# Another order of the steps in each round of the first stage, on four engines

## The reference

```
def bitlinear(x, w, g):
    xn = rmsnorm(x, g)
    xq = ste(xn, act_quant)        # per row: 127 / max|xn|, rounded to integers
    wq = ste(w, weight_quant)      # the weights become -1, 0 or 1, by one scale
    return jnp.einsum('bsd,od->bso', xq, wq)
y = bitlinear(layernorm(x), w_gate, g_gate)        # 512 -> 2 * 1408
gate, v = jnp.split(y, 2, axis=-1)
z = bitlinear(gate * sigmoid(gate) * v, w_down, g_down)      # 1408 -> 512
x = x + z
```

## Time and profile before

| | |
|---|---|
| median of 3 runs | 937.57 us (936.64 to 939.38) |
| profiled execution: span from the first to the last instruction | 967.5 us |
| busy PE, DVE, ACT, POOL over the span | 79%, 52%, 41%, 27% |
| mean granted clock of PE over the span | 0.912 |
| first stage, profiled | to 275.1 us (end of the last `h_lo`) |

### The profile page before, as it was taken

How to read it: one execution, slowest core, us unless ns; L and a number is a source line. 1 busy time by engine, 2 the same in 40 slices (tenths; PEclk the granted TensorE clock), 3 DMA queues, 4 the chain that set the end, 5 groups by cost and what they waited for, 6 DMA issues and landing times.

```text
span 967.5 us, 17562 instructions
## 1 busy us (share of the span) xinstructions
PE 760.4 (79%) x5001; PEld 452.5 (47%) x5017; DVE 504.4 (52%) x861; ACT 397.7 (41%) x567; POOL 263.6 (27%) x401
## 2 busy tenths in 40 slices
PE   0457777777429999749778998899999999999275
PEld 0234443444215555335445655566666666665133
DVE  6779888887714555446564567222222222222146
ACT  5866556656515555335343543122332223231010
POOL 1235665565321111032121000111111111104710
PEclk9979899888559999969898999899999999999679
DMA  9312222212544555267776542122222222226843
GB/s 353 112 34 77 61 70 87 87 66 87 158 159 135 180 179 179 95 209 238 230 215 216 201 148 78 56 88 87 76 77 86 87 78 77 84 77 224 248 138 138
DMA packets 51204, 127.57 MB, mean 132 GB/s; under 512 B 6496, under 2 KB 6496, under 8 KB 50528
## 3 DMA queue, kind: packets, MB, share of 16 engines
q1 hardware_dynamic: 42688, 99.33, 30.5%
q0 software_dynamic: 8480, 27.79, 9.9%
HBM read 87.78 MB, written 39.32 MB: 131 GB/s over the span
## 4 chain that ended last, share of the span: by engine, by line
PE 47%; DMA 10%; issue 4%; another core or an unknown queue 4%; DVE 4%; SPq 2%; ACT 1%; POOL 0%; DVEq 0%; POOLq 0%; ACTq 0%
PE banks L1338 41%; DMA x_d<-w_hi 5%; PE banks L1330 3%; PE banks L1428 2%; DMA x_d<-yrow 2%; DMA hC_d<-w_lo 1%; PE banks L1360 1%; DMA rows<-hC_d 1%; DVE w_hi L1246 0%; DMA rows<-hC_d,idx 0%; SPq L458 0%; SPq L441 0%; DVE w_lo L1102 0%; DMA rows<-hB_d,idx 0%
## 5 line engine op out<-in xcount | busy, mean ns | idle before, releaser
L1338 PE MATMUL banks<-w_hi,hT 128*128 (+1 forms) x1288 | 321.0, 326 | 4.4 <-issue 3.2
L1338 PE MATMUL banks<-w_lo,hT 128*128 (+1 forms) x644 | 209.8, 326 | 0.0
L1338 PEld LDWEIGHTS banks<-w_hi,hT 128*128 128x128 f16 x1288 | 128.0, 99 | 82.2 <-issue 10.6
L1338 PE MATMUL banks<-w_hi,cpT 128*128 (+1 forms) x426 | 142.9, 390 | 10.0 <-issue 8.6
L1299 PE MATMUL banks<-w_hi,w_lo 128*128 128x352 bf16 x384 | 89.3, 350 | 45.6 <-DVE w_hi L1015 34.3
L844 ACT ACTIVATE cs<-banks 128x352 f32<-128x352 f32 x71 | 32.9, 463 | 201.7 <-PE banks L1338 175.5
L1160 DVE TENSOR_TENSOR cs<-banks,cs 128x352 f32<-128x352 f32 x71 | 37.1, 523 | 140.9 <-ACT cs L844 135.0
L1164 DVE TENSOR_TENSOR cpT<-banks,cpT 128x384 f16<-128x384 f32 x71 | 39.5, 556 | 129.3 <-ACT cpT L849 112.6
L1338 PE MATMUL banks<-w_lo,cpT 128*128 (+1 forms) x213 | 83.1, 390 | 5.3 <-issue 5.3
L1330 PE MATMUL banks<-eyeH,rows 128*128 128x128 f16 x584 | 47.6, 225 | 48.2 <-DMA rows<-hC_d 19.6
L1338 PEld LDWEIGHTS banks<-w_lo,hT 128*128 128x128 f16 x644 | 63.9, 99 | 34.5 <-issue 0.8
(11 more groups left out here) (191 smaller groups left out, 1214.3 us busy)
## 6 DMA issues: line engine op xcount, KB each, us to landing
wstage<-in_wmoe SPq DMA_DIRECT2D x40, 544.0 KB
yC_d<-yrow SPq DMA_DIRECT2D x39, 256.0 KB, 2.0
w_hi<-x_d SPq DMA_DIRECT2D x20, 256.0 KB
yB_d<-yrow SPq DMA_DIRECT2D x19, 256.0 KB, 2.0
w_hi<-in_wgate SPq DMA_DIRECT2D x3, 1408.0 KB, 9.9
w_hi<-in_x SPq DMA_DIRECT2D x16, 256.0 KB, 2.8
w_lo<-in_x SPq DMA_DIRECT2D x16, 256.0 KB, 3.6
x_d<-w_lo SPq DMA_DIRECT2D x16, 256.0 KB, 2.9
```

The costliest lines, as they stand in the source:

```text
L1338: mm = pe.matmul(to, a(k, pa), w(k, pw), start=(begins and k == 0 and n == 0), stop=(ends and k == steps - 1 and n == 2))
```

## The change

Four lists are written in another order: those of POOL, ACT, DVE and PE for the first stage. SP's is as before. The steps, their tiles, their waits and their buffers are the same; the place of the second stage's weight chunks in the lists of ACT and DVE moves too.

```diff
@@ POOL
-            pipeline(pool, T, [(-2, small_x), (1, small_g), (3, small_b), (0, lambda s: gains(s, 0)),
-                               (0, lambda s: gains(s, 1)), (3, h_lo)])
+            pipeline(pool, T, [(-2, small_x), (3, small_b), (1, small_g), (0, lambda s: gains(s, 0)), (3, h_lo),
+                               (0, lambda s: gains(s, 1))])
@@ ACT
-            stages = [(0, lambda s: silu(s, 0)), (2, d_evac), (0, lambda s: silu(s, 1)), (1, square), (-1, dequant_x),
-                      (0, lambda s: silu(s, 2)), (-1, x_evac), (-2, x_round), (1, dequant_g),
-                      (0, lambda s: silu(s, 3)), (1, d_round), (3, h_hi)]
+            stages = [(0, lambda s: silu(s, 0)), (1, square), (0, lambda s: silu(s, 1)), (2, d_evac), (-1, dequant_x),
+                      (1, dequant_g), (1, d_round), (0, lambda s: silu(s, 2)), (-1, x_evac), (-2, x_round), (3, h_hi),
+                      (0, lambda s: silu(s, 3))]
-            pipeline(act, T, stages[:8] + [ctx_chunks(ctx_split)] + stages[8:], begin=CTX_FROM)
+            pipeline(act, T, stages[:10] + [ctx_chunks(ctx_split)] + stages[10:], begin=CTX_FROM)
@@ DVE
-            stages = [(3, residual1), (0, lambda s: swiglu(s, 0)), (1, g_absmax), (-3, x_spread),
-                      (0, lambda s: swiglu(s, 1)), (-1, x_int), (3, spread1), (-3, x_moments), (-2, x_reciprocal),
-                      (3, moments1), (-2, x_factor), (0, lambda s: swiglu(s, 2)), (1, g_reciprocal), (3, norm1),
-                      (1, g_factor), (-3, x_center), (0, lambda s: swiglu(s, 3)), (-3, x_absmax), (1, d_int)]
+            stages = [(3, residual1), (0, lambda s: swiglu(s, 0)), (3, spread1), (3, moments1), (1, g_absmax),
+                      (0, lambda s: swiglu(s, 1)), (-3, x_spread), (-3, x_moments), (1, g_reciprocal), (1, g_factor),
+                      (-2, x_reciprocal), (-2, x_factor), (-1, x_int), (3, norm1), (0, lambda s: swiglu(s, 2)), (1, d_int),
+                      (-3, x_center), (-3, x_absmax), (0, lambda s: swiglu(s, 3))]
@@ PE
             stages = [(0, lambda s: gate_up(s, 0)), (0, lambda s: gate_up(s, 1)), (2, d_turn),
-                      (0, lambda s: gate_up(s, 2)), (2, down), (-1, x_turn), (0, lambda s: gate_up(s, 3))]
+                      (0, lambda s: gate_up(s, 2)), (-1, x_turn), (2, down), (0, lambda s: gate_up(s, 3))]
```

## The result

The changed kernel takes **967.0 us** (median of 4 runs, 965.77 to 970.45) against 937.1 for the one before on the same chip (4 runs, 934.96 to 939.38): 1.0316 times as long, with a 95% interval of 1.0287 to 1.0346. The prediction was 961, within 934 to 975, with 0.72 for slower.

A forecast was written before the change was run, and what follows sets the result against it. The prediction took a cycle of waits to set the round, now through a late `x_int` and idle PE. Rounds and stage end gave -0.5 us, the clock +24: 937.6 + 23.5 = 961 us, range 934 to 975.

The forecast's parts named there:

- The walk of the cycle: First-stage round: `x_int`, held by `gains` 0, ends at 7.8 us, PE idles from 3.3; 13.15 us at full clock against 13.18.
- The clock: PE's clock falls after each round's 4.5 us idle piece, over `down` and `gate_up` 3: 2.0 us a round, +24 in all.
- A: Rival: DVE's relief sets the first-stage round at about 11.6 us, 915 us in all; chance 0.17, including a part of it.
- B: Rival: the walk holds but PE's clock does not fall, or falls only where it did before: 937 us; chance 0.12.
- C: Rival: `x_int` is not held, the round is 0.8 us shorter, the clock still falls: 951 us; chance 0.10.
- D: Rival: the whole PE chain runs at half clock, 6.7 us low each round: 974 us; chance 0.13 with what lies near.
- The sum: First-stage parts together -0.5 us without the clock, +24 for the clock: +23.5 us, later stages only moved.
- round 1: First stage's first round: `x_int` now waits for `small_g` and `gains` 0 too, while the clock is low: about +2.5 us.
- round 2: First stage's second round, without `small_b`: 12.2 us against 11.21, +1.0, plus half a clock loss for a shorter idle piece.
- rounds 3 to 12: First stage's middle rounds: 131.5 us at full clock against 131.33, +0.2 with the clock left out.
- rounds 13 to 15: First stage's last rounds, two without `small_x` or `x_int`: 37.1 us against 36.73, +0.4 without the clock.
- after the last `swiglu` 3: End of the first stage: its first piece falls from 15.4 us to about 10.8, -4.6; the 16.8 of loads stays.

The follow-up runs named there:

- e3: Changed kernel with 34 unused matmuls of 256 columns ahead of `x_turn`'s wait for `x_int`, from tile 2 on: 941.9 us, 1.005 times the kernel before.
- e1: Changed kernel with `x_int` moved behind `x_moments` on DVE, ahead of the wait for `small_g`: 926.3 us, 0.987 times the kernel before.
- e2: Changed kernel with `down` ahead of `x_turn` on PE, as in the kernel before: 922.8 us, 0.984 times the kernel before.
- e9: e7 with `swiglu` 3 right behind `swiglu` 2 on DVE, and ACT's `x_evac` and `h_hi` ahead of `silu` 2: 981.0 us, 1.012 times the kernel before.
- e7: Changed kernel with the edits of e1 and e2, and `norm1` ahead of the wait for `small_g`: 951.2 us, 0.982 times the kernel before.
- e4: Kernel before with `x_int` moved from behind `swiglu` 1 to behind `g_factor` on DVE: 982.6 us, 1.046 times the kernel before.
- e5: Kernel before with `x_turn` ahead of `down` on PE: 966.5 us, 0.997 times the kernel before.
- e11: Changed kernel timed again, unaltered, on the chip of e9: 998.6 us, 1.031 times the kernel before.

## Why the prediction was right

**The walk of the cycle** ended with `x_int` at 7.8 us after `swiglu` 3; the trace has 7.99. The hold was 0.29 beyond the `gains` (0.27 expected), `x_int` 1.20 (1 to 1.4), PE's idle piece 4.82 (4.5). The round at full clock was forecast as 13.15 and e3 measured 13.22. This was the step on which all else stood, and e1 and e2 show that it was the cause, since either way out of it removes the whole loss. The Trainium skill ("SBUF — State Buffer", section "Who interferes with whom") says that the later of the two instructions is blocked until the earlier one is through. The trace agrees for `x_int`, which started 0.76 us into the `gains` and ended 0.29 after it, while the `gains` kept its 1.67. It does not agree for `x_center` in e9: there the `gains` had started first and still took 2.05.

**The clock** was priced at 2.0 us a round; e3 gives 2.08. That this is so close is in part luck: 2.0 was a choice between 0 and 4, made for one kind of round, and there are two. The rounds take 14.7 to 14.8 and 15.9 in turn, some 1.6 and 2.7 over e3's, and 2.08 is the mean of the eight. `down` takes 3.50 us in the shorter, as in one of them (timeline of PE), and 4.47 in the longer, as above:

```profile
151.33 0.61 PE L1285 MATMUL banks<-w_lo 128*128 128x128 bf16 x4 [4.83 <-DVE w_lo L1007]
152.15 3.50 PE L1316 MATMUL banks<-w_lo 128*128 128x512 bf16 x10 [0.22 <-issue]
```

**The rivals.** A, that DVE's relief sets the round at 11.6, fell with the rounds of 15.3. With PE's wait out of the way (e2) the round is 11.83, near its number, but not shown to be so for its reason: e7 frees DVE of the last held `norm1`, DVE is busy 9.5 us a round there, and the round stays at 11.91. B fell with the clock at 0.83. C fell with `x_int` at 1.20. D's 974 would need rounds near 16.2; they are 15.3.

**The sum**, part by part, in us (before, after, difference, and what was forecast):

| part | before | after | difference | forecast |
|---|---|---|---|---|
| round 1 | | | +3.5 | +2.5 |
| round 2 | 11.21 | 14.93 | +3.7 | +2.0 |
| rounds 3 to 12 | 131.33 | 153.36 | +22.0 | +20.2 |
| rounds 13 to 15 | 36.73 | 42.68 | +5.95 | +3.4 |
| after the last `swiglu` 3 | 32.74 | 26.50 | -6.2 | -4.6 |
| first stage | | | +28.95 | +23.5 |

The measured time is 6 us above the forecast, 5.5 of them in this table: four parts were put too small and one too large, and the mechanism stands. Rounds 1 and 2 are ordinary long rounds: I had given round 2 only 1.0 for its waits. In rounds 13 to 15 I left out that without `small_x` the others of POOL's list still wait for `g_absmax`; `x_int` of 256.19 is held 1.56 us, PE idles 4.37 ahead of it and `down` takes 4.47:

```profile
256.19 1.56 DVE L1007 TENSOR_SCALAR w_lo<-w_lo 128x512 bf16<-128x512 f32 x1
...
257.81 0.61 PE L1285 MATMUL banks<-w_lo 128*128 128x128 bf16 x4 [4.37 <-DVE w_lo L1007]
258.63 4.47 PE L1316 MATMUL banks<-w_lo 128*128 128x512 bf16 x10 [0.22 <-issue]
```

The ten middle rounds were put 0.18 each too short, of which the walk is 0.07 and the clock 0.08. The end of the stage was 1.6 better than forecast. From 28.95 to the 29.9 of the medians is 1 us, which the later stages may have added or which is noise. That the span of before stands 29.9 above its median was carried over "unchanged", which came out right only because the sum was a difference; the profiled execution of after has no such offset.

## What to carry to other kernels

When steps are reordered to free an engine from holds, ask which operation now stands behind a late wait or beside the other engine's long one, and who is queued behind whoever waits for it; one step moved out of that meeting was worth 41 us here (e1), and one moved from behind the waiting step 44 (e2). An idle piece of PE ahead of a chain on the critical path is paid for twice, in the wait and in the clock; price the two apart, and test the clock with dummy matmuls that change no wait. When the busiest engine gets faster and the time doesn't, look for the wait that took over before looking for another bound.

## What the runs showed that I had not expected

`x_center`, an operation of DVE with two inputs from SBUF and f32 on both sides, is held beside a `gains` as well: 2.16 us in the median for 0.74, with the `gains` itself slowed from 1.67 to 2.05 (e9). In the held `x_int` cases the `gains` kept its 1.67. The trace of before already has one such case: the longest of its 16 `x_center` took 1.91 us.

The clock can be held up by work that does nothing: 34 matmuls a round kept it at 1.00 over all eight rounds where the kernel itself had 0.83, and this was worth 25 us. They ran in time in which PE had stood idle: of its 4.82 us ahead of `x_turn`, 1.10 are left. They gave no gain against the kernel before (1.0045, an interval of 1.0019 to 1.0072), since the wait for `x_int` remained.

The kernel before took 937 us beside the changed kernel and beside e1 to e4, and 969 to 970 on the two chips of e5 to e11, with ScalarE standing 22 to 29 us in the last stage in the profiles from there. The ratio of the changed kernel to it was untouched (1.0316 and 1.0314).
